# Member sums by TensorE, row numbers by VectorE, dense combination weights and a delayed run of unread products in a routed transformer block

## The reference

```
g = t @ gate_w.T + gate_b                 # 16 logits a token
top_vals, top_idx = top_k(g, 4)
route_w = softmax(top_vals)
comb = einsum('nke,nk->ne', one_hot(top_idx, 16), route_w)
h1 = einsum('nh,ech->nec', t, mlp1_w) + mlp1_b
a = swiglu(h1)
y = einsum('nec,ehc->neh', a, mlp2_w) + mlp2_b
out = x + einsum('neh,ne->nh', y, comb)
```

## Time and profile before

| | us |
|---|---|
| median of 3 runs | 506.99 (506.65 to 512.21) |
| the profiled execution | 506.39 |
| its span in the trace | 504.6 |
| lies around the span | 1.8 |
| mean granted clock of TensorE | 0.936 |

### The profile page before, as it was taken

One profiled execution on the slowest core, in us unless ns is written; L12 is line 12 of the kernel. 1 busy time (PEld: TensorE's weight loads), 2 busy tenths in 40 slices (PEclk: granted clock), 3 DMA queues, 4 the chain that ended last, 5 costly groups with the idle time before them and its releaser, 6 DMA issues.

```text
span 504.6 us, 10757 instructions
## 1 busy us (share of the span) xinstructions
PE 404.8 (80%) x2983; PEld 281.0 (56%) x2983; DVE 309.6 (61%) x829; ACT 261.2 (52%) x617; POOL 251.3 (50%) x218
## 2 busy tenths in 40 slices
PE   0455469799999978481699999999999999999920
PEld 0341126666665645230377777777777777777710
DVE  0576776577888887220266776677666666676610
ACT  0639873556667553000356665666566656665510
POOL 7887830000365666656045455555555565555540
PEclk9999996999999997777699999999999999999985
DMA  8999952700122222271234444444444444444335
GB/s 230 252 248 246 270 150 59 213 2 18 33 85 68 85 84 85 83 196 68 79 42 67 69 81 68 69 75 74 68 68 76 73 69 68 68 73 76 42 42 116
DMA packets 43283, 49.66 MB, mean 98 GB/s; under 512 B 7835, under 2 KB 34717, under 8 KB 43229
## 3 DMA queue, kind: packets, MB, share of 16 engines
q1 hardware_dynamic: 25006, 29.93, 23.5%
q0 software_dynamic: 16256, 17.38, 20.3%
q10 hardware_dynamic: 1966, 1.66, 1.2%
HBM read 29.41 MB, written 21.35 MB: 101 GB/s over the span
## 4 chain that ended last, share of the span: by engine, by line
PE 51%; DMA 20%; SPq 11%; DVE 7%; issue 4%; POOL 3%; ACT 1%; POOLq 0%; ACTq 0%; DVEq 0%
DMA xs<-R 16%; PE pair L1258 12%; PE pair L1247 5%; PE pair L1236 5%; PE pair L1240 5%; PE pair L1237 5%; PE pair L1239 5%; PE pair L1238 5%; SPq L266 3%; PE pair L1219 3%; SPq L267 2%; DMA W2s<-in_m 2%; SPq L265 2%; POOL xs L354 2%; PE pair L1261 1%
## 5 line engine op out<-in xcount | busy, mean ns | idle before, releaser
L705 DVE TENSOR_SCALAR R<-pair 128x384 f32<-128x384 f32 x79 | 44.1, 558 | 91.6 <-PE pair L1240 91.6
L368 POOL DMA_INDIRECT out<-R x40 | 64.4, 1610 | 65.7 <-ACT R L946 65.7
L368 POOL DMA_INDIRECT acc_odd<-R x39 | 62.7, 1608 | 52.7 <-ACT R L946 52.7
L354 POOL DMA_INDIRECT xs<-R x64 | 62.7, 980 | 37.2 <-DMA xs<-R 28.8
L1258 PE MATMUL pair<-W2s,R 128*128 x711 | 71.6, 246 | 0.8 <-ACT R L946 0.8
L934 ACT ACTIVATE R<-pair 128x384 f32<-128x384 f32 x79 | 38.8, 491 | 60.2 <-PE pair L1240 60.2
L1258 PEld LDWEIGHTS pair<-W2s,R 128*128 128x128 f16 x711 | 60.6, 98 | 2.1 <-issue 1.0
L928 ACT ACTIVATE R<-pair 128x384 f16<-128x384 f16 x79 | 38.1, 483 | 40.1 <-PE pair L1219 40.1
L315 POOL DMA_INDIRECT R<-in_x,idx_sb x42 | 51.4, 1224 | 13.6 <-issue 12.5
L1240 PE MATMUL pair<-W1s,R 67*128 x158 | 52.2, 330 | 0.0
L1236 PE MATMUL pair<-W1s,R 128*128 x158 | 52.1, 330 | 0.0
(11 more groups left out here) (237 smaller groups left out, 764.2 us busy)
## 6 DMA issues: line engine op xcount, KB each, us to landing
R<-xs SPq DMA_DIRECT2D x79, 104.5 KB, 2.0
W1s<-in_m1a SPq DMA_DIRECT2D x14, 384.0 KB
W2s<-in_m SPq DMA_DIRECT2D x14, 288.0 KB
W1s<-in_m1c SPq DMA_DIRECT2D x14, 192.0 KB
acc_odd<-lz SPq DMA_DIRECT2D x17, 96.0 KB, 1.8
W1s<-W1s SPq DMA_DIRECT2D x1, 1536.0 KB, 10.1
out<-h_all SPq DMA_DIRECT2D x8, 192.0 KB, 2.2
out<-acc_odd POOLq DMA_DIRECT2D x1, 1536.0 KB, 10.7
```

What stands on the lines that cost most here:

```text
L354: po.indirect_dma_start(out=xs, out_offset=bass.IndirectOffsetOnAxis(ap=sl_i[:, q, n:n + 1], axis=0), in_=rowb[:, q, j, :], in_offset=None ...
L368: po.indirect_dma_start(out=(out, acc_odd)[t % 2], out_offset=bass.IndirectOffsetOnAxis(ap=li, axis=0), in_=yv[:, t % 4, :], in_offset=Non ...
L705: ve.tensor_scalar(lin[:, p, :], bank[2 + 2 * p][:, 0:HID], (LIMIT + 1) * S1, (1 - LIMIT) * S1, ALU.min, ALU.max).then_inc(s_lin, 1)
```

## The change

- GpSimd's additions, its memset of `Mall` and its copies of row numbers go. Its loop is now: wait for the slots, eight scatters. The number of scatters in flight stays two (`WAYS` = 2), and the counting rewritten with `scattered()` gives the same wait values as before.
- `low_rows(b)` (VectorE) copies the row numbers of batch b, ahead of its two subtractions.
- `ranks(b)` adds 2b products over the members of all earlier tiles (32 columns each) in place of two over `Mall`, and waits for the members alone. `counts()` runs 16 products of 16 columns in place of 3.
- `ew` is dense: ScalarE takes the exponential of all 16 logits less the top one. `weights` becomes: multiply with `Mx`, sum, reciprocal, one scaling into `rowb`. The 128-element multiplication and reduction go.
- Stages 5 and 6 of the attention end in 4 unread products in place of 5.
- The unread products before the tiles are 28 in place of 40, and start only once scatter 57 (counted from 0; 58 have been issued by then) has landed.

```diff
+WAYS = 2
-                if b < NB - 1:
-                    po.wait_ge(s_mr, b + 1)
-                    po.tensor_tensor(Mall[:, b + 1, :], Mall[:, b, :], Mx[:, 2 * b, :], ALU.add).then_inc(s_ma, 1)
-                    po.wait_ge(s_ma, 2 * b + 2)
-                    po.tensor_tensor(Mall[:, b + 1, :], Mall[:, b + 1, :], Mx[:, 2 * b + 1, :], ALU.add).then_inc(s_ma, 1)
-                    po.wait_ge(s_ma, 2 * b + 3)
                 po.wait_ge(s_sl, b + 1)
-                po.tensor_copy(rowb[:, q, :, D + NE:D + NE + 1].bitcast(I32),
-                               idx_sb[:, 42 + 2 * b:42 + 2 * b + 2].rearrange("p (t n) -> p t n", n=1)).then_inc(s_idr, 1)
-                po.wait_ge(s_idr, b + 1)
...
-                        wait(po, s_sct[n % 2], 16 * (4 * b + n // 2))
+                        i = 8 * b + n
+                        wait(po, s_sct[i % WAYS], 16 * scattered(i, i % WAYS))
...
             def low_rows(b):
                 ve.wait_ge(s_th, b + 1)
                 r2 = rows[:, b % BUFS, :, :]
+                ve.tensor_copy(rowb[:, b % BUFS, :, D + NE:D + NE + 1].bitcast(I32),
+                               idx_sb[:, 42 + 2 * b:42 + 2 * b + 2].rearrange("p (t n) -> p t n", n=1))
...
-                ve.tensor_tensor(ew[:, p, :, :], mx8[:, :, 0:TOPK], mx8[:, :, 0:1].broadcast_to([P, 2, TOPK]),
+                ve.tensor_tensor(ew[:, p, :, :], g_all[:, 2 * b:2 * b + 2, :], mx8[:, :, 0:1].broadcast_to([P, 2, NE]),
                                  ALU.subtract).then_inc(s_nx, 1)
...
-                link(ve, ve.tensor_reduce(es[:, :], ew[:, p, :, :], AX.X, ALU.add))
+                link(ve, ve.tensor_tensor(cw[:, :, :], ew[:, p, :, :], Mx[:, 2 * b:2 * b + 2, :], ALU.mult))
+                link(ve, ve.tensor_reduce(es[:, :], cw[:, :, :], AX.X, ALU.add))
                 link(ve, ve.reciprocal(es[:, :], es[:, :]))
-                link(ve, ve.scalar_tensor_tensor(out=ew[:, p, :, :], in0=ew[:, p, :, :], scalar=1.0 / (SA * S2),
-                                                 in1=es[:, :].rearrange("p (t k) -> p t k", k=1).broadcast_to([P, 2, TOPK]),
-                                                 op0=ALU.mult, op1=ALU.mult))
-                link(ve, ve.tensor_tensor(ohw[:, :, :, :], oh[:, p],
-                                          ew[:, p, :, :].rearrange("p t (k e) -> p t k e", e=1).broadcast_to(full), ALU.mult))
-                ve.tensor_reduce(rowb[:, b % BUFS, :, D:D + NE], ohw[:, :, :, :].rearrange("p t k e -> p t e k"), AX.X,
-                                 ALU.add).then_inc(s_cb, 1)
+                ve.scalar_tensor_tensor(out=rowb[:, b % BUFS, :, D:D + NE], in0=cw[:, :, :], scalar=1.0 / (SA * S2),
+                                        in1=es[:, :].rearrange("p (t k) -> p t k", k=1).broadcast_to([P, 2, NE]),
+                                        op0=ALU.mult, op1=ALU.mult).then_inc(s_cb, 1)
...
             def ranks(b):
                 pe.wait_ge(s_mr, b + 1)
-                pe.wait_ge(s_ma, 2 * b + 1)
...
+                for t in range(2 * b):
+                    mm(o, ones16, Mx[:, t:t + 1, :].broadcast_to([P, 2, NE]), start=False, stop=False)
                 mm(o, ustrict, Mx[:, 2 * b:2 * b + 2, :].rearrange("p t e -> p (t e)"), start=False, stop=False)
-                for j in range(2):
-                    mm(o[:, NE * j:NE * (j + 1)], ones16, Mall[:, b, :], start=False, stop=False)
...
-                pe.wait_ge(s_ma, 2 * NB - 1)
...
+                for t in range(NT):
+                    ins = mm(o, ones16, Mx[:, t, :], start=t == 0, stop=t == NT - 1)
+                ins.then_inc(s_cn, 1)
...
-                    keep_busy(bank[0], 8 if s == 0 else 5)
+                    keep_busy(bank[0], 8 if s == 0 else 5 if s < 5 else 4)
...
-            keep_busy(bank[1], 40)
+            n = 8 * NB - 7
+            pe.wait_ge(s_sct[n % WAYS], 16 * (n // WAYS + 1))
+            keep_busy(bank[1], 28)
```

More of the change, by code:

```diff
@@ L180, in build @@
         mx8, ix8 = carve([2, 8]), carve([2, 8], U32)
-        ew, es = carve([2, 2, TOPK]), carve([2])
+        ew, es, cw = carve([2, 2, NE]), carve([2]), carve([2, NE])
         ohw = carve([2, TOPK, NE])
-        Mx, Mall = carve([NT, NE], F16), carve([NB, NE], F16)
+        Mx = carve([NT, NE], F16)
         sl_i = carve([BUFS, 8], I32)
@@ L231, in build @@
         s_nx = sem("s_top_negated"); s_ex = sem("s_top_exp"); s_cb = sem("s_comb_ready")
-        s_mr = sem("s_members"); s_ma = sem("s_members_summed"); s_rp = sem("s_rank"); s_ru = sem("s_rank_used"); s_sl = sem("s_slots")
-        s_idr = sem("s_row_numbers"); s_sct = [sem(f"s_rows_scattered{k}") for k in range(2)]
+        s_mr = sem("s_members"); s_rp = sem("s_rank"); s_ru = sem("s_rank_used"); s_sl = sem("s_slots")
+        s_sct = [sem(f"s_rows_scattered{k}") for k in range(WAYS)]
         s_cn = sem("s_counts"); s_pr = sem("s_pad_starts"); s_pad = sem("s_pads_stored")
@@ L247, in wait, with scattered @@
                 eng.wait_ge(s, v)
+        def scattered(n, k):
+            return (n + WAYS - 1 - k) // WAYS
         NCONST = 3 * 16
@@ L297, in _ @@
             sp.wait_ge(s_pad, 16 * (NE + 1))
-            for k in range(2):
-                sp.wait_ge(s_sct[k], 16 * 4 * NB)
+            for k in range(WAYS):
+                sp.wait_ge(s_sct[k], 16 * scattered(8 * NB, k))
             for t in range(STEPS):
@@ L352, in _ @@
                         n = TOPK * j + k
-                        wait(po, s_sct[n % 2], 16 * (4 * b + n // 2))
+                        i = 8 * b + n
+                        wait(po, s_sct[i % WAYS], 16 * scattered(i, i % WAYS))
                         po.indirect_dma_start(out=xs, out_offset=bass.IndirectOffsetOnAxis(ap=sl_i[:, q, n:n + 1], axis=0),
-                                              in_=rowb[:, q, j, :], in_offset=None).then_inc(s_sct[n % 2], 16)
+                                              in_=rowb[:, q, j, :], in_offset=None).then_inc(s_sct[i % WAYS], 16)
             po.wait_ge(s_tab, 1)
-            for k in range(2):
-                po.wait_ge(s_sct[k], 16 * 4 * NB)
+            for k in range(WAYS):
+                po.wait_ge(s_sct[k], 16 * scattered(8 * NB, k))
             po.memset(Cb[D1:67, :, :], 1.0).then_inc(s_ms, 1)
@@ L861, in high_rows @@
                 ac.wait_ge(s_tp, b + 1)
-                for k in range(2):
-                    wait(ac, s_sct[k], 16 * 4 * (b - BUFS + 1))
+                for k in range(WAYS):
+                    if b >= BUFS:
+                        ac.wait_ge(s_sct[k], 16 * scattered(8 * (b - BUFS + 1), k))
                 ac.activation(rows[:, b % BUFS, :, 0:D], tp, ACT.Copy).then_inc(s_th, 1)
@@ L1152, in counts @@
                 pe.wait_ge(s_mr, NB)
-                pe.wait_ge(s_ma, 2 * NB - 1)
                 pe.wait_ge(s_qe, NB)
                 o = bank[3][:, 0:NE]
-                mm(o, ones16, Mall[:, NB - 1, :], start=True, stop=False)
-                mm(o, ones16, Mx[:, NT - 2, :], start=False, stop=False)
-                mm(o, ones16, Mx[:, NT - 1, :], start=False, stop=True).then_inc(s_cn, 1)
+                for t in range(NT):
+                    ins = mm(o, ones16, Mx[:, t, :], start=t == 0, stop=t == NT - 1)
+                ins.then_inc(s_cn, 1)
             for b in range(6):
```

2 lines of the change are left out of this document (removed).

## The result

| | before | after |
|---|---|---|
| median, us | 509.3 (504.79 to 513.13, 20 runs) | 504.01 (499.32 to 510.04, 20 runs) |
| ratio to before, 95% interval | | 0.9887 [0.9858, 0.9915] |
| span of the profiled execution | 504.6 | 503.9 |
| GpSimd, instructions | 218 | 195 |
| first scatter issued | 134.22 | 137.19 |

The kernel is 5.3 us faster by medians, 1.1% by the ratio; by that ratio the forecast's base of 506.99 would have become 501.3. The forecast was 500.1 with a range to 503.0. Two things separate it from 504.01.

The account below looks back on a forecast made before the run. Landings of the 64 scatters into `xs` were taken to set the pace, with GpSimd's own work limiting between batches. Start 1.0 plus boundaries 1.2, 1.0 and 3.7 gave 6.9 us off the median of 506.99: 500.1, range 497.0 to 503.0.

Parts of the forecast that it names:

- What bounds, and where the change works: Scatters into `xs`: landings set the pace, 1.39 us each; between batches GpSimd's own program limits, where the change works.
- The boundaries: Seven steps between batches of scatters: removing GpSimd's small work saves 1.2, twice 0.5, and 3.7 at four, 5.9 us in all.
- the second boundary: Batch 2 to 3, landing late: step from landing to issue falls from 0.73 to 0.27, 0.5 us off.
- the four plain ones: Four boundaries like batch 3 to 4, without late landing: 0.93 us each, 3.7 in all, bounds 3.3 and 4.2.
- The start: First scatter: shorter weights and no GpSimd copy bring it 1.0 us earlier, bounds 0.6 and 1.1.
- Slots in time: Attention stages against scatters: slots come in time, stages 11.8 us, batches at least 11.1, the margin grows; no stall.
- The clock: TensorE between unread products and tiles: clock falls again, gain 0, bounds a gain of 2.1 and a loss of 1.
- The rival that it holds: TensorE's clock stays up into the tiles, 2.1 us more gained, 498.0 us; chance 0.2.
- Counts, pad stores, small products on TensorE at nothing: TensorE's extra products hidden; counts, pad stores and table some 7 us sooner but covered by the scatters: zero gain.
- The rival of hidden landings: Landings that boundaries wait for take 3.1 us, hidden by GpSimd's work: gain 3.4, time 503.6; chance 0.12.
- Crowded landings: Scatters without pauses crowd the DMA engines; landings 0.5 us longer would make 516 us, slower than before; chance 0.04.
- Its own signs: Right: boundary steps near 1.4. Wrong: steps near 2, pace inside batches above 1.39 without pads, clock 1.00, pauses on slots.

Follow-up runs that it names:

- e14: Changed kernel with a one-element GpSimd memset at each batch's head taking the wait for the slots; 502.85 us, 0.9914 of the kernel before.
- e7: Changed kernel with the row numbers copied by GpSimd again, between slots' wait and scatters; 506.43 us, 0.9957 of the kernel before.
- e8: Changed kernel with the combination weights of the kernel before (five linked steps); 505.54 us, 0.9953 of the kernel before.
- e10: Changed kernel unaltered, compared again with the kernel before; 504.19 us, ratio 0.9904.
- e12: Changed kernel unaltered, in a further comparison with the kernel before; 505.41 us, ratio 0.9908.
- e2: Kernel before with only the unread products changed: 28 waiting for scatter 57 in place of 40 at once; 0.9982 of the kernel before.
- e5: Changed kernel with three scatters in flight in place of two, on a chip with pauses; 517.41 us, 1.0130 of the kernel before.
- e4: Changed kernel with the two waits ahead of a batch's first scatter swapped, landing first, then slots; 1.000 of the kernel before.
- e13: Changed kernel with three scatters in flight in place of two, on a chip without pauses; 493.68 us, 0.9670 of the kernel before.
- e6: Changed kernel with four scatters in flight in place of two; 518.16 us, 1.0110 of the kernel before.
- e9: Changed kernel with four scatters in flight and 33 delayed products in place of 28; 516.89 us, 1.0100 of the kernel before.
- e17: Changed kernel with four scatters in flight, slots' wait on a memset for the last two batches, 31 unread products; 489.33 us, 0.9606 of before.
- e3: Changed kernel with 35 delayed unread products in place of 28; 0.9961 of the kernel before.
- e15: Changed kernel with the slots' wait on a GpSimd memset and 35 unread products in place of 28; 499.71 us, 0.9817 of the kernel before.

## Why the prediction was off

*What bounds, and where the change works*: right. The landings' share stayed, GpSimd's work between batches went, and the gain came at the boundaries.

*The boundaries*, forecast 5.9, measured 4.8 (17.4 to 12.6 in the profile). This is the step of the mechanism that failed. The forecast read the 0.73 between a late landing and the issue as a longer step of the first scatter after a copy, and let it fall to 0.27 with the copy. The changed kernel has no copy and still has 0.73. In the kernel before, the scatter behind the copy waited for the copy and for a landing; in the changed one it waits for slots and for a landing. It was the pair of waits, not the copy. The kernel before's chain of waits had it at a boundary without a late landing, from the fourth batch to the fifth:

```profile
187.69 0.02 POOLq L247
187.71 0.01 issue
187.72 0.20 POOL R L347
187.91 0.53 issue
188.44 0.98 POOL xs L354
```

The wait for the landing (line 247) is an instruction of its own there too, and from its end to the scatter's issue pass 0.73, in which the copy runs; the 0.54 behind the copy, which the forecast put down to it, is what it left of these 0.73. At all seven boundaries of before they are 0.73. e14 shows the 0.27. Seven times 0.46 is 3.2; the sum is short by only 1.1 because the second boundary, with the late landing of the earlier trace rows, gained 1.60 (3.55 to 1.95) where 0.5 was told, and the fourth and the seventh each 0.3 more than their terms less 0.46. The 1.60 is for the most part one landing, 4.39 before and 2.76 after. That it fell there is luck as far as the forecast goes, as nothing in it said so; the other kernels with two waits and no pauses (e7, e8, e10 to e12) have 1.86 to 2.22 at this boundary, e2 3.08, and why was not tried. At the four plain ones 0.93 was expected and 0.41, 0.77, 0.41 and 0.50 came.

*The start*, forecast 1.0, measured 0.59, just under the lower bound. The weights were sized right (0.44 in the rows, 0.45 by e8, for 0.5), the copy on VectorE at its lower bound (0.08). The copy on GpSimd was not: the forecast gave its removal 0.7 to 0.8 and kept a surplus of 0.43 as a doubt. The doubt was right in its size: the lag went from 1.05 to 0.84, not to 0.27. GpSimd's long rest ahead of it is not the main cause, as far as shorter ones tell: GpSimd idle for 5.84 us gives 0.28 with the slots' wait written first (e5), idle for 6.11 us 0.78 with it written second (e4). In the first batch no landing is waited for, but the scatter carries the wait for a memset ahead of the loop, and the slots' wait (line 342, at 136.38) is the instruction of its own. So this too fits the wait written second; with a memset first it was 0.87 (e14). What the last 0.07 are was not tried.

*Slots in time*: right in the profile, with less to spare than "the margin grows" says. The lags after are 0.84, 1.33, 2.57, 2.94, 4.16, 5.39, 8.46 and 17.16 (before: 1.05, 3.11, 5.95, 6.51, 8.04, 8.56, 10.85, 13.77). By these lags, an estimate, a pause of 3 us ahead of the third or fourth batch's slots is hidden before, where some 5 us are to spare, as the pauses of e2 were, and delays the scatters after, where 2.3 and 2.7 are. On the two chips that have pauses, ratios are 0.996 to 1.000 for all kernels close to the changed one. This is a price of the change that the forecast did not see.

*The clock*, forecast 0 with bounds -1 and +2.1: right. The products left 2.81 idle (2.3 to 3.7 told), the clock fell and rose later than before, a loss of 0.7 in the profile, and tails of 260.4 and 260.8 in e12 and e10, a gain of some tenths. The rival that it holds needs more products, and is then worth what was said: 258.8 to 258.9 against 260.4 to 261.8, for 2.1.

*Counts, pad stores, small products on TensorE at nothing*: right.

*The rival of hidden landings*: wrong in its cause, and near the time with its 503.6 by luck: its gain was 3.4 where 5.3 to 5.8 came, and the base's 2.3 made up for it. In the batches 89.0 us before became 89.5, and the landings that boundaries wait for took 2.41 and 2.76 in the chain above, not 3.1. The Trainium skill's figures (page DMA: Bandwidth & Descriptors, section Anatomy of one DMA — SWDGE (gpsimd) path) made an estimate of 2.25; the shortest in the whole chain after, 2.40, is above it, so going by the rows was right. *Crowded landings*: not here, nor with four in flight.

*Its own signs*: the one of being wrong, boundary steps near 2, is what the profile showed (five of seven from 1.78 to 1.95). The other, a pace inside the batches above 1.39, says nothing of the change: seven steps without pads took 10.0 to 11.4 us, which is 1.43 to 1.63 a step, and 1.38 to 1.62 in the kernel before. The forecast's 1.39, from undisturbed landings, is reached in two of the sixteen batches.

*The base*: the median of three runs lay 2.3 below that of twenty; the sum was taken off a number that was itself uncertain by as much as a third of the gain. Of the 3.9 us between forecast and time, 2.3 are the base and 1.6 the gain, and either alone would have left the time below 503.0. That bound is itself mis-added: its terms, 0.4, 0.4, 1 and 0.6, lead from 500.1 to 502.5.

## What to carry to other kernels

An issue step after a wait is a measurement of that form of instruction: before its excess is booked to the work ahead of it, count how many waits it has. If it has two, write first the one that will be met last, or give the early one to a cheap instruction of its own. When a serial chain of landings is shortened, ask again what stands behind it; here the next limit, VectorE's stages, was 1 to 3 us away at the second to fourth batch, and with four scatters in flight it set the pace up to the sixth. And a result of 1% belongs to a chip until a second one has shown it.

## What the hardware showed that was not expected

- An indirect scatter with two waits on GpSimd is issued 0.77 us after the one written second, where that is met last (landings in after, slots in e4), and 0.27 after the one written first (slots in e5, landings in e4). With one wait it is 0.27 (e14).
- One source took 1.013 of the time of before on one chip and 0.967 on another (e5, e13), with pauses of VectorE of 1 to 6 us on the first only. The one of line 577 ended with TensorE's signal, 5.61 us after the products' recorded end, where on the other chip it is 0.02. Ahead of the second batch the pause is 3.37, 3.38 and 3.37 us in e5, e6 and e9.
- With four indirect scatters of 107 KB in flight GpSimd issues one every 1.27 us, 0.96 busy and 0.30 between, and only two scatters were held up by a landing (e17).
- The same 42 gathers took 51.4 and 57.4 us of GpSimd in two executions of untouched code; in the second the attention was 3.56 us later at its first gates.
- The clock stayed up over idle stretches of 1.23 and 1.84 us ahead of the tiles (e3, e15) and was down after 2.81 and more. In e13 it fell 2.2 us into the tiles although only 1.03 had been idle ahead of them; this is not explained.
